# Four edits to a four-stage conditional MLP kernel: two loads and the bias sums in other places, and another order of the first products

## What is computed

```python
x = x + L0(x)   # shared MLP + the top 2 of 8 skills, each gelu(x Wg) * (x Wu) Wd, 1024 hidden
x = x + L1(x)   # one expert by argmax: (silu(x Wup + bup) * (x Wgate + bgate)) Wdown + bdown, 512 hidden
x = x + L2(x)   # x (sum_g y_g W_g * mask)^T + bias
x = x + L3(x)   # x Wbase^T + b_base + (lora: sum_e w_e B_e (A_e x)) * 2
```

## Time and profile before

| | us |
|---|---|
| median of 3 timed runs | 504.29 (503.1 to 504.32) |
| the profiled execution | 500.07 |
| its span, first to last instruction | 498.4 |
| TensorE busy | 479.7 |
| VectorE busy | 396.5 |
| ScalarE busy | 275.1 |
| GpSimd busy | 33.7 |

### The profile page before, as it was taken

One profiled execution on the slowest core, in us unless ns is written; L12 is line 12 of the kernel. 1 busy time (PEld: TensorE's weight loads), 2 busy tenths in 40 slices (PEclk: granted clock), 3 DMA queues, 4 the chain that ended last, 5 costly groups with the idle time before them and its releaser, 6 DMA issues.

```text
span 498.4 us, 6830 instructions
## 1 busy us (share of the span) xinstructions
PE 479.7 (96%) x2166; PEld 397.2 (80%) x2166; DVE 396.5 (80%) x699; ACT 275.1 (55%) x453; POOL 33.7 (7%) x56
## 2 busy tenths in 40 slices
PE   8999389999999999799999999999999999999997
PEld 7788367888888888678888888888888888888886
DVE  7799169888788789488997988898887799974555
ACT  5567057666646464346563758665766456554442
POOL 1914100000000001020000011000000100000000
PEclk9999969999999999989999999999999999999999
DMA  6989944223309028943356007032229512100002
GB/s 165 218 231 227 144 91 123 66 62 98 94 1 192 19 66 109 173 120 103 89 124 129 0 16 217 27 102 64 64 66 176 141 63 67 61 2 0 0 1 84
DMA packets 112907, 47.33 MB, mean 95 GB/s; under 512 B 66456, under 2 KB 111640, under 8 KB 112872
## 3 DMA queue, kind: packets, MB, share of 16 engines
q1 hardware_dynamic: 109728, 41.30, 36.0%
q0 software_dynamic: 2560, 5.21, 4.3%
q10 hardware_dynamic: 584, 0.39, 0.3%
HBM read 44.79 MB, written 2.10 MB: 94 GB/s over the span
## 4 chain that ended last, share of the span: by engine, by line
PE 76%; DMA 7%; SPq 7%; DVE 6%; issue 2%; ACT 1%; POOL 0%; ACTq 0%; DVEq 0%
PE bank_a L1678 6%; PE bank_a L1680 6%; PE bank_a L1679 6%; PE bank_b L1678 6%; PE bank_b L1680 6%; PE bank_b L1679 6%; PE tail L1702 3%; PE tail L1703 3%; PE tail L1706 3%; DMA raw<-in_L_cond_skill_down 3%; SPq L512 3%; PE out L1702 3%; PE bank_a L1945 3%; PE out L1706 3%; PE out L1703 3%; PE bank_a L1946 3%
## 5 line engine op out<-in xcount | busy, mean ns | idle before, releaser
L711 ACT ACTIVATE hid_hi<-hid 128x512 fp32r<-128x512 f32 x84 | 53.0, 631 | 86.9 <-DVE hid L1010 53.8
L1018 DVE TENSOR_TENSOR hid_lo<-hid,hid_hi 128x512 fp32r<-128x512 f32 x84 | 57.7, 687 | 17.7 <-ACT hid_hi L711 17.6
L1010 DVE SCALAR_TENSOR_TENSOR hid<-bank_b,mine,hid 128x512 f32<-128x512 f32 x64 | 47.6, 743 | 17.9 <-PE bank_b L1680 16.4
L703 ACT ACTIVATE hid<-bank_a 128x512 f32<-128x512 f32 x68 | 40.4, 593 | 37.3 <-PE bank_a L1680 36.3
L999 DVE TENSOR_TENSOR res_lo<-raw,res_hi 128x768 fp32r<-128x768 f32 x36 | 34.2, 951 | 13.8 <-ACT res_hi L690 13.8
L690 ACT ACTIVATE res_hi<-raw 128x768 fp32r<-128x768 f32 x36 | 30.2, 839 | 15.0 <-DMA raw<-in_L_cond_skill_down 14.9
L999 DVE TENSOR_TENSOR w_lo<-raw,w_hi 128x768 fp32r<-128x768 f32 x30 | 28.5, 950 | 1.4 <-ACT w_hi L690 1.4
L1678 PE MATMUL bank_a<-x_hi,res_hi 128*128 128x512 f32 x74 | 28.8, 390 | 0.0
L1679 PE MATMUL bank_a<-x_lo,res_hi 128*128 128x512 f32 x74 | 28.8, 390 | 0.0
L1680 PE MATMUL bank_a<-x_hi,res_lo 128*128 128x512 f32 x74 | 28.8, 389 | 0.0
L1678 PE MATMUL bank_b<-x_hi,res_hi 128*128 128x512 f32 x74 | 28.8, 389 | 0.0
(11 more groups left out here) (356 smaller groups left out, 1320.9 us busy)
## 6 DMA issues: line engine op xcount, KB each, us to landing
raw<-in_L_cond_skill_down SPq DMA_DIRECT2D x64, 128.0 KB, 3.3
raw<-in_L_cond_skill_gate SPq DMA_DIRECT2D x31, 256.0 KB, 3.1
raw<-in_L_cond_skill_up SPq DMA_DIRECT2D x31, 256.0 KB, 3.4
raw<-in_L_cond_shared_down SPq DMA_DIRECT2D x18, 128.0 KB, 3.7
raw<-in_L_cond_shared_gate SPq DMA_DIRECT2D x8, 256.0 KB, 3.2
raw<-in_L_cond_shared_up SPq DMA_DIRECT2D x8, 256.0 KB, 3.6
raw_gate<-in_L_cond_W_gate SPq DMA_DIRECT2D x16, 128.0 KB, 3.2
early<-in_L_cond_weight POOLq DMA_DIRECT2D x2, 1024.0 KB, 10.2
```

Source lines behind the costliest of these rows:

```text
L703: nc.scalar.activation(hid[:, tile_of(g)], bank_a[tile_of(g)][:, :], func, **kw).then_inc(act_ready, 1)
L711: nc.scalar.activation(hid_hi[:, tile_of(g)], hid[:, tile_of(g)], ACT.Copy).then_inc(hid_hi_ready, 1)
L1010: ins = nc.vector.scalar_tensor_tensor(tile, bank, weight, tile, ALU.mult, ALU.mult)
L1018: nc.vector.tensor_tensor(hid_lo[:, tile], hid[:, tile], hid_hi[:, tile].bitcast(F32), ALU.subtract).then_inc(hid_lo_ready, 1)
```

## The change

1. The load of L1's W_up for batch 0, `first_l1(2)`, is issued behind joint chunk 4 and W_down instead of behind joint chunk 2 and W_gate.
2. `bias_base` is run in the sixth pair unit of batch 0, `bias_lora` and `bias_columns` behind L1's fourth chunk in batch 1, where `bias_base` was; they were behind chunks 6 and 7 of batch 1.
3. The first `ca_product` goes with chunk 7 instead of 6, and both it and the second one are issued ahead of the down products instead of behind them.
4. The start: x's second half is issued by ScalarE behind the first weight rows; SyncE waits for the first routing step before the second rows. GpSimd rounds the first rows and makes their low part. TensorE's warm-up is six products of 512 columns on ones, and four of 128 behind the first transposes; x's second transposes and the routing's product stand behind the first two products. ScalarE copies x (`x0_copied`) beside chunks 1 and 2 instead of in chunk 0.

```diff
-PREPS = ["x", "route"]
+PREPS = ["route", "x"]
-FILL = 2
+FILL = 4
-CA_PLACE = {6: 0, 14: 1}
+CA_PLACE = {7: 0, 14: 1}
-BIAS_LORA_AT = 6
-BIAS_AT = 7
+BIAS_BASE_IN = 5
+X0_COPY_AT = 1
@@ SyncE
-            for k in range(KD):
-                cols = slice(k * P, (k + 1) * P)
-                sp.dma_start(x_nat[:, 0, :, cols], x_rows[0][:, :, cols]).then_inc(x0_in[k], 16)
-                if k:
-                    first_rows(k)
+            sp.dma_start(x_nat[:, 0, :, 0:P], x_rows[0][:, :, 0:P]).then_inc(x0_in[0], 16)
+            sp.wait_ge(route_step, 1)
+            first_rows(1)
                 if (kind, b, c) == ("joint", 0, 2):
                     first_l1(0)
-                    first_l1(2)
                 if (kind, b, c) == ("joint", 0, 4):
                     first_l1(1)
+                    first_l1(2)
@@ GpSimd
+            first_part = raw[:, raw_slot(0), 0:4:2, 0:P]
+            pool.wait_ge(first_in[0], 32)
+            nc.gpsimd.tensor_copy(res_hi[:, 0, 0:4:2], first_part).then_inc(first_hi[0], 1)
+            pool.wait_ge(first_hi[0], 1)
+            nc.gpsimd.tensor_tensor(res_lo[:, 0, 0:4:2], first_part, res_hi[:, 0, 0:4:2].bitcast(F32), ALU.subtract)\
+                .then_inc(first_lo[0], 1)
@@ ScalarE
                     if i == 0:
                         hidden_hi(0, i)
-                        for k in range(KD):
-                            nc.scalar.activation(out_pair[:, k], tail[:, k, :], ACT.Copy).then_inc(x0_copied, 1)
                     if i + SPLIT_AHEAD <= UNIT_AT[0]:
                         split(0, i + SPLIT_AHEAD)
                     if i:
                         hidden_hi(0, i)
+                    if 0 <= i - X0_COPY_AT < KD:
+                        k = i - X0_COPY_AT
+                        nc.scalar.activation(out_pair[:, k], tail[:, k, :], ACT.Copy).then_inc(x0_copied, 1)
+            act.dma_start(x_nat[:, 0, :, P:2 * P], t["x"].rearrange("b (q p) d -> b p q d", q=NQ)[0][:, :, P:2 * P])\
+               .then_inc(x0_in[1], 16)
@@ VectorE
                 elif c == 3:
                     x_turn_blocks(3)
-                    bias_base()
+                    bias_lora()
+                    bias_columns()
-                    if i == BIAS_LORA_AT:
-                        bias_lora()
-                    if i == BIAS_AT:
-                        bias_columns()
                 hidden(b, n, weight=mine[:, 1:2])
+                if unit == BIAS_BASE_IN:
+                    bias_base()
-            first_parts(0)
             first_x_parts(0)
+            take_chosen()
             first_parts(1)
             first_x_parts(1)
@@ TensorE
                     for bank, n in banks:
                         nc.tensor.matmul(bank, hi[:, n + k], x_hi[:, k, cols], start=k == 0, stop=False)
-                    pe.wait_ge(first_lo, k + 1)
+                    if k == 0:
+                        route()
+                        turn_first_x(1)
+                    pe.wait_ge(first_lo[k], 1)
                     l0_gate_up(b, i)
+                    if i in CA_PLACE:
+                        ca_product(CA_PLACE[i])
-                    if i in CA_PLACE:
-                        ca_product(CA_PLACE[i])
+                    nc.tensor.matmul(out0[:, 0, 0:cols], filler[:, 0:P], filler[:, 0:cols], start=True, stop=True)
-            turn_first_x()
-            route()
+            turn_first_x(0)
+            fill(FILL, P)
             first_head()
```

More of the change, by code:

```diff
@@ L281, in build @@
         wpart = sb("wpart", [B, 2])
-        warm = hid[:, 0, 0:P]
-        filler = xs_hi[:, 0, 0:P]
+        filler = xs_hi[:, 0, :]
         pick_diag = sb("pick_diag", [B, B, PICK])
@@ L367, in build @@
         x0_copied = sem("x0_copied")
-        first_hi = sem("first_hi")
-        first_lo = sem("first_lo")
+        first_hi = [sem(f"first_hi{k}") for k in range(KD)]
+        first_lo = [sem(f"first_lo{k}") for k in range(KD)]
         first_x_lo = sem("first_x_lo")
@@ L977, in _ @@
             nc.scalar.activation(x_hi[:, 0, 0:S], tail[:, 0, :], ACT.Copy).then_inc(x_hi_ready, 1)
-            act.wait_ge(tail_ready, 1)
+            act.wait_ge(tail_ready, PREPS.index("x") + 1)
             nc.scalar.activation(x_hi[:, 1, 0:S], tail[:, 1, :], ACT.Copy).then_inc(x_hi_ready, 1)
@@ L1619, in pair_rest @@
                         turn_chunk(b, REST_TURN[i])
-            nc.vector.memset(warm, 0.0).then_inc(warm_ready, 1)
             nc.vector.memset(filler.bitcast(F32), 1.0).then_inc(warm_ready, 1)
@@ L1637, in first_parts @@
                 dve.wait_ge(first_in[k], 32)
[L1638 to L1641, removed]
+                nc.vector.tensor_copy(res_hi[:, 0, k:4:2], part).then_inc(first_hi[k], 1)
+                dve.wait_ge(first_hi[k], 1)
                 nc.vector.tensor_tensor(res_lo[:, 0, k:4:2], part, res_hi[:, 0, k:4:2].bitcast(F32), ALU.subtract)\
-                    .then_inc(first_lo, 1)
+                    .then_inc(first_lo[k], 1)
             def first_x_parts(k):
@@ L1718, in first_gate_up @@
                 for k in range(KD):
-                    pe.wait_ge(first_hi, k + 1)
+                    pe.wait_ge(first_hi[k], 1)
                     pe.wait_ge(x_hi_ready, k + 1)
@@ L1744, in l0_down @@
                     pe.wait_ge(split_lo, 1)
-                    pe.wait_ge(tail_free, PREPS.index("route") + 1)
+                    pe.wait_ge(tail_free, len(PREPS))
                 if (b, i) == (JOINT, 0):
@@ L1884, in closing, with turn_first_x @@
                 low_rows(1)
[L1886 to L1895, removed]
+            def turn_first_x(k):
+                pe.wait_ge(x0_in[k], 16)
+                for q in range(NQ):
+                    ins = nc.tensor.transpose(tail[:, k, q * P:(q + 1) * P], x_nat[:, 0, q, k * P:(k + 1) * P], ident[:, :])
+                ins.then_inc((x0_turned, tail_ready)[k], 1)
             def route():
@@ L2047, in pair_rest, with fill @@
                         ca_product(b)
-            def warm_up(times):
+            def fill(times, cols):
                 for _ in range(times):
-                    nc.tensor.matmul(out0[:, 0, 0:P], warm, warm, start=True, stop=True)
-            def fill(times):
-                for _ in range(times):
-                    nc.tensor.matmul(out0[:, 0, 0:P], filler, filler, start=True, stop=True)
+                    nc.tensor.matmul(out0[:, 0, 0:cols], filler[:, 0:P], filler[:, 0:cols], start=True, stop=True)
             pe.wait_ge(warm_ready, 1)
-            warm_up(WARM)
-            pe.wait_ge(warm_ready, 2)
+            fill(WARM, S)
             pe.wait_ge(const_pool, 2)
             pe.wait_ge(const_dve, 1)
-            turn_first_x()
-            route()
+            turn_first_x(0)
+            fill(FILL, P)
             first_head()
```

## The result

| | before | after |
|---|---|---|
| median of 4 timed runs | 504.31 us | 486.30 us (484.49 to 488.44) |
| the profiled execution | 500.07 | 488.44 |
| its span | 498.4 | 486.7 |
| TensorE busy | 479.7 | 477.2 |

The ratio is 0.9648, 95% interval 0.9606 to 0.9691: 18.0 us faster, where 18.2 were forecast (486.1 us). What follows from a trace alone has to be read with that in mind.

A forecast was written before the change was run, and what follows sets the result against it. The end is set by TensorE's own queue of products, so time is won only where it stands still. Gains 12.0 + 5.5 + 0.3 + 0.4 = 18.2 us; 504.29 - 18.2 = 486.1 us, range 481 to 493.

The forecast's parts named there:

- Stop A: TensorE's wait for ScalarE's hidden-chunk rounding, near 54 us, 9.8 plus 2.7 at low clock; moving W_up gains 12.0 us.
- if GpSimd's queue wins again: Upper bound for TensorE's wait left near 54 us, should GpSimd's loads delay chunks 12 and 13: 3 us.
- The pair W_down and W_up: Both loads together between joint chunk 4 and own chunk 14, ending at 56 to 71 us: cost 0.
- Rivals 3 and 4: W_down and W_up loads delay own chunk 14 (496.8 us, chance 0.06), or L1's weight turning, slower than before (506, 0.03).
- rival 5: Chunks 12 and 13 are held by SyncE's full queue, the wait near 54 us stays: 498.1 us, chance 0.04.
- Stop B: TensorE's wait for VectorE's output rows, in slice 17, 3.8 plus 1.7 us at low clock; moving bias sums gains 5.5.
- the bias columns near 162: Sign expected in the profile after: bias columns near 162 us, with no VectorE wait on the sums.
- What is next late there is nothing: With the output-rows wait gone, nothing else in TensorE's waits was expected to be late there.
- rival 2: Bias rows still late, small writes running beside the second batch's L1 loads: 491.6 us, chance 0.05.
- The second folded product: Batch 1's CA product swaps with a down product of 1.4 us; its a2 low part is there 0.7 before: cost 0.
- The start: First product 0.75 us earlier, mostly given back; the 0.4 us wait for first skill weights can be won: gain 0.4.
- The bound of 1.8 us: Cost at the first products if the clock stayed low up to 10 us; taken as cost 0.

The follow-up runs named there:

- the second trace: The changed kernel run again, unedited, beside later experiments: median 483.8 us, ratio to the kernel before 0.9655.
- W_gate behind too: Changed kernel with W_gate's load for batch 0 issued behind own chunk 12 instead of behind joint chunk 2: 483.4 us, ratio to before 0.9645.
- the old start: Changed kernel with the start of the kernel before, the three other edits kept: 483.9 us, ratio to before 0.9640.
- the second product back: Changed kernel with the second folded product (ca_product of batch 1) behind chunk 14's down product again: 482.6 us, ratio to before 0.9627.
- the folded products alone: Kernel before with only the ca_product moves: first one chunk later, both ahead of the down products: 501.8 us, ratio to before 0.9989.
- the start alone: Kernel before with only the new start, the change's fourth point with all its parts: 502.0 us, ratio to before 0.9977.

## Why the prediction was right, and where it wasn't

**Stop A: right alone, landing later in company.** Forecast 12.0, measured alone 11.8. Issue (39.46), landing (51.07) and the absence of a new stop are as it had them there. In the changed kernel the chunks went out at 41.57 and 42.55 and their split waited until 55.45 and 53.59, so one of the prediction's own signs of being wrong was met (ScalarE waits for skill weights past 52). The bound of 3 us "if GpSimd's queue wins again" is what the first trace of the changed kernel shows (1.7 + 0.6 us and some wide spacing), the second trace shows 0.2. What holds the chunks in those 11 to 14 us is in part W_gate in front of them, as moving it took 2 to 5 us off, and in part GpSimd's two loads, beside which SyncE's queue moved nothing from 42 to 44 us once W_gate was out of the way. The prediction's premises for the landing were other ones: no hold of SyncE for these issues (they took 5.1 us in all alone and 6.0 in the changed kernel, 2.3 without W_gate in front), and packets of the two queues in turns, which that stretch doesn't show. So it is in part luck that the landing came out right alone.

**The pair W_down and W_up: right at 0.** In the changed kernel the first turning of L1's weights stands at 77.89 with no wait, and own chunk 14 lands in time. Rivals 3 and 4 are not seen in any trace, nor is rival 5: the chunks go out 0.16 or 0.17 us after the low part of chunk 9 that frees their slot, in every kernel with W_up moved.

**Stop B: mechanism right, term mis-sized.** Forecast 5.5, measured alone 7.4. The step that failed is the first sentence of it, 3.8 + 1.7 from one execution: four executions gave 5.3 + 2.2 in the mean. A stop that a DMA ends has no single length. The way from step to arrival was forecast at 18.8 and took 171.9 to 191.3, 19.4 us; the output at 196.63 didn't wait. One number was worked out wrongly: "the bias columns near 162". 180.6 less the 12 us won before is 168.6; the traces have 171.9 and, in the trace with the least lost (W_gate behind too), 167.6.

**"What is next late there is nothing": wrong.** The prediction moved the small writes in front of SyncE's loads for L1 and priced what this does to the bias rows (rival 2), not what the rows do to the loads. It had the row for it: the wait of 10.40 us for 4 KB. Price: 2.6 us of waits in one trace, 1.2 in another and none in the three others that keep both places, not measurable in the medians.

**The second folded product: "cost 0" holds only when nothing else is late.** Alone it makes no wait; behind late skill weights it made one of 1.5, with the old start 1.2. The margin of 0.7 us that the prediction read was the whole cover.

**The start: right at about 0.** First product forecast at 5.75, found at 6.16; GpSimd's two steps forecast at 0.6 and 0.9, found at 0.40 and 0.73 (1.7 times VectorE's 0.43), but the weights landed at 5.35 and not at 5. The first chunk was to end at about 9.5 as before: the second one starts at 10.05 (before 9.52), and the wait of 0.4 for the skill weights is gone. So 14.24 against 14.22 at the third group of products, in the trace; 1.2 us alone by the ratio, nothing in company. One reading was wrong: "the page shows the full clock for the first slices". The page can't show it, since the record of the clock begins late (last section); in the kernel before the products stood at the wide spacing until 5.3 us. The bound of 1.8 us that the prediction gave for a low clock there was met in two traces.

**The sum.** The parts alone add up to 20.9 us (plus or minus 2.9), together they gave 18.0 and 17.3 (each plus or minus 2.1); the intervals don't separate them. That the 18.2 came so near was in part luck: stop B was 1.9 too small, and the traces have some of that left in new and remaining waits, 2.9 and 7.8 us lost in the two of the changed kernel against 0.6 at best. The excess of 4.2 us of the timed runs over the profiled one was taken as a constant. It isn't one: the first trace of after has it with the other sign (488.44 against 486.3). Some 2 us of it were the short stop B of that execution. The rest is mostly of that group of runs: the four of before lie 1.9 to 3.3 us above the medians of the same kernel beside the experiments, and the four of after lie 2.5 above its later median. As both kernels had it, the forecast of 486.1 met 486.3; beside the experiments 483.8 was measured. What made that group slower stays open.

## To carry to other kernels

Before a small write or a load with short runs is moved, ask what stands behind it in every queue: 4 KB in 1024 pieces held large loads of another queue for their whole 10 us. Count a stop that a transfer ends from several traces, since one gave 3.8 where the mean was 5.3. And give work that is moved ahead of another product more cover than the margin read in one trace, or it takes up the first delay that comes along.

## What the runs showed that was not expected

**GpSimd stops VectorE beside it.** Timelines of GpSimd and VectorE at the start of the changed kernel:

```profile
5.37 0.40 POOL L596 CAST res_hi<-raw 128x256 fp32r<-128x256 f32 x1 [3.76 <-DMA raw<-in_L_cond_shared_up]
5.85 0.73 POOL L598 TENSOR_TENSOR res_lo<-raw,res_hi 128x256 fp32r<-128x256 f32 x1
...
5.42 0.36 DVE L1329 COPY pick<-logits 4x8 f32<-4x8 f32 x1
...
5.88 0.76 DVE L1333 TENSOR_TENSOR pick_diag<-pick,ident 4x52 f32<-4x52 f32 x1
```

In the kernel before these two took 0.15 and 0.20 us. Here they end with GpSimd's instructions or just behind them: 5.78 and 5.77, 6.64 and 6.58. In the second trace, where GpSimd's subtraction ran from 5.41 to 6.13, the copy took 0.64 and ended at 6.16, and pick_diag, begun behind it, took 0.20. The Trainium skill (SBUF — State Buffer, "Who interferes with whom") says that a VectorE instruction with two inputs in SBUF contends with a GpSimd one that reads SBUF. The subtraction's effect on pick_diag, which has two inputs, agrees with it; the copy has one, so that sentence doesn't cover it. It looks like the reason for the later choice of experts (7.28 instead of 6.36, and with it the first skill load at 8.45 instead of 7.53), but it isn't: pick_diag ended at 6.64 here and at 6.46 in the kernel with the second product back, and the routing's product came at 6.79 and 6.80, 0.32 and 0.33 us behind the second main product. The order of TensorE's products sets the choice, as the prediction had it.

**The first products have two speeds.** In the trace of the folded products alone, whose start is that of the kernel before:

```profile
7.85 0.63 PE L1725 MATMUL bank_a<-x_hi,res_lo 128*128 128x512 f32 x1
8.28 0.63 PE L1725 MATMUL bank_b<-x_hi,res_lo 128*128 128x512 f32 x1
8.71 0.63 PE L1728 MATMUL bank_a<-x_lo,res_hi 128*128 128x512 f32 x1
```

0.43 us apart, where before had 0.23; from 10.4 us on they are 0.23 apart. The new start had it too, in the trace of the start alone, up to 10.9 us. 0.43 is the spacing behind stop A, where the granted clock was at its low level. In this stretch the view of windows gives a granted clock of 1.00, but that is no measurement: the trace's record of the clock begins only at 10.34 us, at 10.96 in the start alone, at 5.32 in the kernel before and at 6.10 in the changed one, and the views count the time ahead of it as full. In all fourteen traces the record begins (4.2 to 11.0 us) where the spacing halves, from 0.21 to 0.11 us for 128 columns or from 0.43 to 0.23 for 512. So TensorE starts at the low level in all of them, and they differ in when it rises. It cost 1.8 us here (14.22 became 16.03) and 2.1 with the new start (the first group of down products ends with a start at 15.72, not 13.67), as large as the prediction's bound for it. What TensorE did before doesn't tell the traces apart: this one and the kernel before have the same products up to 5.2 us, and the clock rose at 5.3 in one and 10.3 in the other. What decides it stays open.
